# Query features interleaved over the partitions and moved in three wide transfers, row maxima turned by one transpose

## The reference

```python
# layer 0: differential attention, 32 half-heads of 8, softmax over 77 keys
q = layernorm(x) @ Wq.T; k = ctx @ Wk.T; v = ctx @ Wv.T
att = softmax(einsum('bhtd,bhnd->bhtn', q, k) * 8 ** -0.5)      # 32 half-heads
att = att[:, :, 0] - lam * att[:, :, 1]                          # 16 heads
x = x + tanh(g) * einsum('bhtn,bhnd->bhtd', att, v)
x = x + tanh(g) * (mixture of top 3 of 8 experts, gelu)(layernorm(x))
# layer 1: 16 heads of 16, the same Wq (with its bias) for q, k and v
att = softmax(einsum('bhqd,bhkd->bhqk', q, k) / 4)
x = x + tanh(g) * ((att @ v) @ Wo + bo)
x = x + tanh(g) * (silu(h @ Wg) * (h @ Wu)) @ Wd                 # h = layernorm(x)
```

## Time and profile before

| | |
|---|---|
| median of 3 runs | 671.64 us (671.02 to 672.87) |
| the profiled execution's own time | 671.35 us |
| its span in the trace | 669.6 us |
| TensorE (PE) busy | 608.3 us, 91% |
| VectorE (DVE) busy | 384.5 us, 57% |
| ScalarE (ACT) busy | 361.6 us, 54% |
| GpSimd (POOL) busy | 148.2 us, 22% |
| mean granted TensorE clock | 0.985 |

### The profile page before, as it was taken

How to read it: one execution, slowest core, us unless ns; L and a number is a source line. 1 busy time by engine, 2 the same in 40 slices (tenths; PEclk the granted TensorE clock), 3 DMA queues, 4 the chain that set the end, 5 groups by cost and what they waited for, 6 DMA issues and landing times.

```text
span 669.6 us, 11648 instructions
## 1 busy us (share of the span) xinstructions
PE 608.3 (91%) x4364; PEld 503.0 (75%) x4364; DVE 384.5 (57%) x813; ACT 361.6 (54%) x615; POOL 148.2 (22%) x218
## 2 busy tenths in 40 slices
PE   2688888898899999999999999999778998999998
PEld 2565555554599899999999888899656776878887
DVE  6668676887753524434555434534486663656654
ACT  4345757686765746546557435535675433443421
POOL 9716265354630000000000000000564210210000
PEclk9789999999999999999999999999999998999999
DMA  7302120222030030300312340020132100000000
GB/s 226 107 12 88 35 62 8 49 51 97 32 126 1 10 117 1 118 9 1 126 25 72 80 142 2 2 95 2 44 99 65 35 1 0 34 1 22 12 33 31
DMA packets 22551, 34.76 MB, mean 52 GB/s; under 512 B 4704, under 2 KB 13280, under 8 KB 22496
## 3 DMA queue, kind: packets, MB, share of 16 engines
q1 hardware_dynamic: 20224, 30.51, 14.7%
q0 software_dynamic: 1984, 3.44, 2.2%
q10 hardware_dynamic: 288, 0.07, 0.0%
HBM read 18.93 MB, written 2.10 MB: 31 GB/s over the span
## 4 chain that ended last, share of the span: by engine, by line
PE 73%; DVE 10%; ACT 5%; issue 4%; POOL 3%; DMA 1%; ACTq 0%; DVEq 0%; POOLq 0%
PE PV L1259 21%; PE SC L1287 21%; PE SC L1259 9%; PE PV L1278 4%; PE AUX L1259 4%; DVE NM L1134 3%; PE SC L1406 3%; PE AUX L1368 3%; PE PV L1287 2%; PE AUX L1287 2%; DVE O L1142 2%; ACT PB L906 2%; ACT XN L851 1%; PE AUX L1326 1%; POOL RSTD L716 1%
## 5 line engine op out<-in xcount | busy, mean ns | idle before, releaser
L992 DVE TENSOR_TENSOR HL<-HF,HH 128x512 fp32r<-128x512 f32 x96 | 67.2, 700 | 154.6 <-ACT HH L948 154.4
L906 ACT ACTIVATE PB<-SC 77x1024 f32<-77x1024 f32 x96 | 95.2, 1014 | 50.1 <-PE SC L1406 49.8
L1287 PE MATMUL SC<-WBH,HL 128*128 128x256 f32 x384 | 108.7, 283 | 0.0
L1287 PE MATMUL SC<-WBL,HH 128*128 128x256 f32 x384 | 108.6, 283 | 0.0
L1287 PE MATMUL SC<-WBH,HH 128*128 128x256 f32 x384 | 108.6, 283 | 0.0
L948 ACT ACTIVATE HH<-PV 128x512 fp32r<-128x512 f32 x96 | 57.3, 596 | 72.1 <-PE SC L1287 72.1
L943 ACT ACTIVATE HF<-PV 128x512 f32<-128x512 f32 x96 | 57.3, 597 | 54.7 <-PE PV L1259 52.7
L716 POOL TENSOR_TENSOR RSTD<-RSTD,NHALF 128x4 f32<-128x4 f32 x16 | 17.8, 1115 | 291.5 <-DVE RSTD L1066 291.4
L1259 PE MATMUL PV<-XH,WAH 128*128 128x512 f32 x192 | 77.6, 404 | 1.0 <-DVE O L1142 1.0
L1287 PEld LDWEIGHTS SC<-WBL,HH 128*128 128x128 f32 x384 | 72.7, 189 | 3.9
L1287 PEld LDWEIGHTS SC<-WBH,HH 128*128 128x128 f32 x384 | 72.5, 189 | 4.0 <-DVE HL L992 0.3
(11 more groups left out here) (254 smaller groups left out, 1228.7 us busy)
## 6 DMA issues: line engine op xcount, KB each, us to landing
QG<-QH SPq DMA_DIRECT2D x96, 64.0 KB, 2.0
WSA<-in_wa SPq DMA_DIRECT2D x6, 1024.0 KB, 4.8
WSB<-in_wb SPq DMA_DIRECT2D x12, 512.0 KB, 6.4
QG<-QL SPq DMA_DIRECT2D x48, 64.0 KB, 2.0
X<-in_x SPq DMA_DIRECT2D x4, 512.0 KB, 6.0
QG<-QH POOLq DMA_DIRECT2D x32, 64.0 KB, 2.3
out_x<-X SPq DMA_DIRECT2D x8, 256.0 KB, 2.1
QG<-QL POOLq DMA_DIRECT2D x16, 64.0 KB, 2.3
```

The source lines that it names most:

```text
L906: act.activation(probs(n)[0:S, :, :], scores(n)[0:S, :, :], ACT.Exp, scale=SCALE[a]).then_inc(exp_done, 1)
L992: return dve.tensor_tensor(dst, raw, hi.bitcast(F32), ALU.subtract)
L1287: ins = pe.matmul(ps[:, D * (t % 2):D * (t % 2 + 1)], lhs[:, block], rhs, start=first and t == 2 * i and n == 0, stop=last and t == 2 * i ...
```

## The change

1. The columns of both `Wq` (and the bias per feature) are put in another order on the host: feature `4r + g` of a half is row `r` of group `g`. So the four groups of a half lie interleaved over the 128 partitions, and one DMA of 128 rows x 512 fills 32 rows of all four groups. A half takes 3 DMAs in place of 12. In the pairs of `BOTH` the third is issued by GpSimd's queue, which waits for `QH` alone.
2. `NM` has the heads outside and the blocks inside, `NM[:, n % 2, h, t]`, so that one transpose turns heads x blocks (64, 32 or, in attention 1, 32 columns) at once. ScalarE copies a bank of up to 64 rows x 128, and the DMA to `QG` reads 16 (or 8) rows of 128 for each group.
3. `WDH` and `WDL` for layer 1 must have the groups in the old order: the copies and subtractions read `WQ1R` with a step of four elements, four instructions each in place of one on ScalarE and two on GpSimd. The products of `keys(1, 3)` and `keys(1, 4)` read `WQ1H` and `WQ1L` with a step of four elements as moving operand.

```diff
         SG = [at(f"SG{i}", [P, NT], F32, wq_at + 4096 + 2048 * i) for i in range(2)]
-        NM = place("NM", [P, 2, TT, HEADS[0]], F32)
-        NMT = place("NMT", [P, NT], F32R)
+        NM = place("NM", [P, 2, HEADS[0], TT], F32)
+        NMT = place("NMT", [P, P], F32R)
         ident = place("ident", [P, P], F32)
...
         def query_moved(eng, n, c):
-            eng.wait_ge(q_moved[n % 2][c], 16 * sum(6 if m in BOTH else 12 for m in range(n % 2, n + 1, 2)))
+            eng.wait_ge(q_moved[n % 2][c], 16 * sum(2 if m in BOTH else 3 for m in range(n % 2, n + 1, 2)))
             if n in BOTH:
-                eng.wait_ge(pool_moved[n][c], 16 * 6)
+                eng.wait_ge(pool_moved[n][c], 16)
+
+        def by_group(raw, c, h):
+
+            return (raw[:, c, P * h:P * (h + 1)].rearrange("p (r g) -> p g r", g=G // KC)
+                    .unsqueeze(2).to_broadcast([P, G // KC, 3, 32]))
         def ffn_half(i, h):
...
                 return ap.rearrange("(c p) n -> p c n", p=P)
+
+            def move_maxima(queries, a, g, at_g):
+
+                return sp.dma_start(queries[ROWS:ROWS + NS[a], g, :].bitcast(F32),
+                                    NMT[at_g:at_g + NS[a] * TT, :].bitcast(F32))
             sp.dma_start(X[:, 0:TT, :], x[0]).then_inc(x_in[0], 16)
...
                     used(sp, ("query", a, j, c))
-                    for r in range(2 if n in BOTH else 4):
-                        for q, src in enumerate((QH, QL, QH)):
-                            sp.dma_start(QG[n % 2][32 * q:32 * q + 32, 4 * c + r, :].bitcast(F32),
-                                         src[32 * r:32 * r + 32, c, :].bitcast(F32)).then_inc(q_moved[n % 2][c], 16)
+                    for q, src in enumerate((QH, QL) if n in BOTH else (QH, QL, QH)):
+                        sp.dma_start(QG[n % 2][32 * q:32 * q + 32, G // KC * c:G // KC * (c + 1), :].bitcast(F32),
+                                     src[:, c, :].bitcast(F32)).then_inc(q_moved[n % 2][c], 16)
                 elif kind == "negmax":
...
                     for g in range(G // KC):
-                        at_g = 32 * c + NS[a] * g
-                        sp.dma_start(QG[n % 2][ROWS:ROWS + NS[a], G // KC * c + g, :].bitcast(F32),
-                                     NMT[at_g:at_g + NS[a], :].bitcast(F32)).then_inc(m_moved[n % 2][G // KC * c + g], 16)
+                        move_maxima(QG[n % 2], a, G // KC * c + g,
+                                    64 * c + NS[a] * TT * g).then_inc(m_moved[n % 2][G // KC * c + g], 16)
                 elif kind == "negpart":
...
                     for g in (2 * p, 2 * p + 1):
-                        at_g = 64 * p + NS[0] * (g % 2)
-                        sp.dma_start(QG[0][ROWS:ROWS + NS[0], g, :].bitcast(F32),
-                                     NMT[at_g:at_g + NS[0], :].bitcast(F32)).then_inc(m_moved[0][g], 16)
+                        move_maxima(QG[0], 0, g, 64 * p + NS[0] * TT * (g % 2)).then_inc(m_moved[0][g], 16)
                 elif kind == "zone_load":
...
                         pool.wait_ge(sc_ready, unit((n - 2) // J, (n - 2) % J, 0) + units[(n - 2) // J] * (c + 1) // KC)
-                    used(pool, ("query", a, j, c))
-                    for r in range(2, 4):
-                        for q, src in enumerate((QH, QL, QH)):
-                            pool.dma_start(QG[n % 2][32 * q:32 * q + 32, 4 * c + r, :].bitcast(F32),
-                                           src[32 * r:32 * r + 32, c, :].bitcast(F32)).then_inc(pool_moved[n][c], 16)
+                    filled(pool, ("query", a, j, c))
+                    pool.wait_ge(qh_ready, order["query", a, j, c] + 1)
+                    pool.dma_start(QG[n % 2][2 * 32:3 * 32, G // KC * c:G // KC * (c + 1), :].bitcast(F32),
+                                   QH[:, c, :].bitcast(F32)).then_inc(pool_moved[n][c], 16)
                 elif kind == "weights_split" and step[1] == 2:
...
                     lo_part(WQ1L[:, :, :], WQ1R[:, :, :], WQ1H[:, :, :]).then_inc(split1_done, 1)
-                    pool.wait_ge(split_hi, 6)
+                    pool.wait_ge(split_hi, 9)
                     for c in range(KC):
-                        lo_part(WDL[:, c, :, :, :],
-                                WQ1R[:, c, :].rearrange("p (g r) -> p g r", r=32).unsqueeze(2).to_broadcast([P, G, 3, 32]),
-                                WDH[:, c, :, :, :]).then_inc(split1_done, 1)
+                        for h in range(KC):
+                            gs = slice(G // KC * h, G // KC * (h + 1))
+                            lo_part(WDL[:, c, gs, :, :], by_group(WQ1R, c, h), WDH[:, c, gs, :, :]).then_inc(split1_done, 1)
                 elif kind == "weights_split" and step[1] == 0:
...
                     filled(act, ("keys", 0, 4, 0))
-                    dup_hi(WQ1R)
+                    for c in range(KC):
+                        for h in range(KC):
+                            act.activation(WDH[:, c, G // KC * h:G // KC * (h + 1), :, :], by_group(WQ1R, c, h),
+                                           copy).then_inc(split_hi, 1)
                 elif kind == "weights_split":
...
                             act.wait_ge(m_moved[(n - 1) % 2][g], 16 * ((n - 1) // 2 + 1))
-                    n_heads = HEADS[a] // KC
-                    act.activation(NMT[32 * c:32 * c + n_heads, :], bank(step + (0,))[0:n_heads, :], copy).then_inc(frees(step + (0,)), 1)
+                    rows = HEADS[a] // KC * TT
+                    act.activation(NMT[64 * c:64 * c + rows, :], bank(step + (0,))[0:rows, 0:P], copy).then_inc(frees(step + (0,)), 1)
                 elif kind == "negpart":
...
                     filled(act, key)
-                    act.activation(NMT[at_p:at_p + 8, :], bank(key)[0:8, :], copy).then_inc(frees(key), 1)
+                    act.activation(NMT[at_p:at_p + 32, :], bank(key)[0:32, 0:P], copy).then_inc(frees(key), 1)
                 elif kind == "attend":
...
                     filled(dve, key)
-                    dve.tensor_reduce(NM[:, n % 2, t, h:h + k], bank(key)[:, 0:k * S].rearrange("p (h n) -> p h n", h=k),
+                    dve.tensor_reduce(NM[:, n % 2, h:h + k, t], bank(key)[:, 0:k * S].rearrange("p (h n) -> p h n", h=k),
                                       AX_X, ALU.max, negate=True).then_inc(frees(key), 1)
...
                 return ins
+            def turn_maxima(ps, maxima):
+
+                rows = maxima.shape[1] * TT
+                return pe.transpose(ps[0:rows, 0:P], maxima.rearrange("p h t -> p (h t)"), ident[:, :])
+
             def attend_values(a, j, k):
...
                         else:
-                            pe.wait_ge(split1_done, 3)
+                            pe.wait_ge(split1_done, 5)
                     ps = fill(step + (0,))
...
                         cols = slice((i - 3) * S, (i - 2) * S)
-                        ins = product(ps[0:S, 0:D], [(CH[:, c, cols], CL[:, c, cols], vh[:, c, :], vl[:, c, :])
-                                                     for c in range(KC)])
+                        if a == 0:
+                            vh, vl = (tuple(w[:, c, :] for c in range(KC)) for w in (vh, vl))
+                        else:
+                            vh, vl = (tuple(w[:, c, :].rearrange("p (k r g) -> p k g r", k=KC, g=G // KC)
+                                            for c in range(KC)) for w in (vh, vl))
+                        ins = product(ps[0:S, 0:D], [(CH[:, c, cols], CL[:, c, cols], vh[c], vl[c]) for c in range(KC)])
                     ins.then_inc(aux_ready, 1)
...
                     ps = fill(step + (0,))
-                    for t in range(TT):
-                        ins = pe.transpose(ps[0:8, P * t:P * (t + 1)], NM[:, 0, t, 8 * p:8 * p + 8], ident[:, :])
-                    ins.then_inc(aux_ready, 1)
+                    turn_maxima(ps, NM[:, 0, 8 * p:8 * p + 8, :]).then_inc(aux_ready, 1)
                 elif kind == "negmax":
...
                     ps = fill(step + (0,))
-                    for t in range(TT):
-                        ins = pe.transpose(ps[0:n_heads, P * t:P * (t + 1)],
-                                           NM[:, (J * a + j) % 2, t, n_heads * c:n_heads * (c + 1)], ident[:, :])
-                    ins.then_inc(aux_ready, 1)
+                    turn_maxima(ps, NM[:, (J * a + j) % 2, n_heads * c:n_heads * (c + 1), :]).then_inc(aux_ready, 1)
                 elif kind == "attend":
...
     bq = np.asarray(inputs["L1_xattn_bq"])
+
+    def by_row(w):
+        return w.reshape(-1, KC, G // KC, 32).transpose(0, 1, 3, 2).reshape(w.shape)
+
     arrays = {
...
         "g_x": inputs["g_xattn"], "g_f": inputs["g_ffn"],
-        "wq0": np.asarray(inputs["L0_xattn_Wq"]).T, "wk0": np.asarray(inputs["L0_xattn_Wk"]).T,
+        "wq0": by_row(np.asarray(inputs["L0_xattn_Wq"]).T), "wk0": np.asarray(inputs["L0_xattn_Wk"]).T,
         "wv0": np.asarray(inputs["L0_xattn_Wv"]).T,
...
         "wa": inputs["L0_ffn_Wa"], "wb": inputs["L0_ffn_Wb"],
```

(8 more changed lines are left out.)

## The result

The changed kernel takes 680.83 us (median of 6 runs) beside 671.46 us for the kernel before (6 runs). One of the six took 1704.97 us, a slow execution; without it the median is 679.94 us, and the ratio, which leaves it out too, is 1.0121, interval 1.0102 to 1.0141: slower by 1.2%, where I had forecast 667.4 us and given slower 0.10. The profiled execution took 681.76 us, its span is 680.0 us, 10.4 us above that of before.

A forecast was written before the change was run, and what follows sets the result against it. It took TensorE to bound the expert stage and a chain changing hands the attentions. Savings of 5.2 us, less 0.55 for the split and 0.5 for strided reads, gave -4.2: 671.64 to 667.4 us, range 664.0 to 671.0.

The forecast's parts named there:

- The query transfers: Query halves moved to QG: each there 1 to 5 us earlier, but hidden; value 0, bounds -0.2 and 0.
- Nothing queued behind the issues on SyncE is late: SyncE's queue: the maxima's transfer starts when its copy ends, so query issues do not delay it; no cost.
- The transfer of the maxima: Maxima's DMA, 1.86 us twice on the chain: 512 B pieces cost between 0 and +0.2 each; taken as 0.
- The transposes and the copies: Maxima on TensorE and ScalarE: fewer transposes save 1.18 and 2.05 us, shorter copies 2.3; 5.2 after taking off 0.3.
- rival 2: Attentions: the next wait takes the savings, only start and expert stage keep theirs; -2.0 us, 669.6 to 670.6; chance 0.19.
- The dearer split: GpSimd's WDL for layer 1: four pieces of 1.04 us, 4.15 against 3.60, +0.55 us straight on the chain.
- Reads with a step of four: The 12 matmuls of keys(1, 3) and keys(1, 4): a doubling, +1.4 us, of which +0.5 on the chain.
- rival 3: Split and layer-1 value products: step-of-four reads are dear, +8.8 against -5.2, 675.2 us, slower; chance 0.10.
- rival 4: TensorE from 42 to 48 us: full clock comes later, up to 5.4 us more, +1.2 net, 672.8 us; chance 0.03.

The follow-up runs named there:

- e8: The changed kernel with its three merged query transfers a half written to every third row of QG, not 32 neighbouring rows; output not the reference's; 669.66 us, ratio 0.9960.
- e3: The changed kernel with each half's queries moved in 12 transfers of 64 KB that read every fourth row; 670.81 us, ratio 0.9978 to the kernel before.
- e1: The kernel before with the turned maxima only (one transpose, copies of 128 columns, maxima's transfers in 512 B rows); 669.71 us, ratio 0.9959.
- e6: e1 with its one transpose done four times over into the same place; ratio 0.9973 to the kernel before.
- e2: The changed kernel without the turned maxima (four transposes and the old copies again); 685.15 us, ratio 1.018 to the kernel before.
- e9: e1 with 16 matmuls of 512 columns, whose result nobody reads, ahead of the first maximum; ratio 0.9964 to the kernel before.
- e10: The kernel before with 16 matmuls of 512 columns, whose result nobody reads, ahead of the first maximum; ratio 1.0007.
- m1: Separate kernel without computation, timing transfers between SBUF rows form by form and in bursts; 256 KB from 128 rows into 32 neighbouring rows took 3.97 us.
- m2: Second transfer-only kernel, with further 256 KB forms differing in rows and piece size; 128 rows into 32 rows that lie four apart took 2.38 us.

## Why the prediction was wrong, step by step

- **The query transfers: this step failed.** "A half is there 1 to 5 us earlier" was wrong in sign for the first half, and with it the value 0. I took the landing of one transfer (3 to 4.5 us; 3.97 measured for one alone) as its whole cost, and forgot that they share the engines: the six of pair 0, both halves, are issued within 3 us, what counts at the start is when the last one of the first half lands, and it took 9.34 us. With the same six in well-spread rows (e8) it took 5.28. My own row gave the warning: the wait of 4.5 us had two causes within 0.15 us of each other, so any growth of the transfer came out one for one. I priced a gain there and no loss. The bounds -0.2 and 0 had no row behind the upper one, since no transfer of this form was in the trace.
- **"Nothing queued behind the issues on SyncE is late".** I looked at when the maxima's transfer is issued, not at what it shares. It landed after 5.28 in place of 1.86 us, +3.4 on the chain. **The transfer of the maxima** by itself was right: 1.96 in e3, +0.1.
- **The transposes and the copies**: the pieces are as forecast (17 in place of 68; 0.27 us; copies 0.26 us against 0.30). Their worth was not: 2.8 us by e1 in place of 5.2. The expert stage gave 1.2 us, what follows 0.6, together the 1.8 by which the span shrank (669.6 to 667.8). In the expert stage I had counted three copies, 0.9 us; e6 shows them at nothing. Attention 0 gave nothing back, the first expert matmul is at 178.9 us in e1 as before, but the savings of its start did appear: at the first key product of layer 1, e1 is 2.03 us ahead (87.93 against 89.96), 0.54 of it by an earlier first maximum. They went again where TensorE ran at the lower clock, as the item on the clock shows. So the sum is near that of rival 2 (-3.0 for transposes and copies), and by luck: rival 2 kept the start's savings and named a second path, not the clock, for the rest.
- **The dearer split**: the term was mis-sized. GpSimd's pieces take 1.18 us and not 1.04, 4.61 against 3.60 us: +1.0 in place of +0.55. The pieces are 14% above my estimate, which took the step of four at nothing; no run has them without the step, so whether the step or the estimate is to blame is not shown.
- **Reads with a step of four** by TensorE: near the doubling that I took. Three of these matmuls in the kernel after start 0.23 us apart, where it was 0.12:

```profile
118.77 0.41 PE L1267 MATMUL PV<-WQ1H,CH 128*77 128x256 f32 x1
119.00 0.41 PE L1267 MATMUL PV<-WQ1L,CH 128*77 128x256 f32 x1
119.23 0.41 PE L1267 MATMUL PV<-WQ1H,CL 128*77 128x256 f32 x1
```

  12 x 0.11 = 1.3 us against my 1.4; the granted clock is 1.00 over these matmuls in both kernels. The rule of the Trainium skill ("Advanced Engine Details and Errata", "Memory Cachelines") that I had weighed is right in sign, and not dear enough for rival 3. Both terms together, +1.05 forecast, are 1.3 us by e3 less e1. The reductions that write `NM` with that step are unchanged (475 and 480 ns in e1, 473 and 479 before).
- **The clock** (rival 4, chance 0.03): it came true in part, beside the main cause. Its sign was a clock below 0.64 behind 27 us. It is 0.50 from 27.6 to 39.5 us in the kernel after, and as low in e1, e3 and e8, which have the turned maxima but no late first maximum, while e6, with four transposes again, has 0.64. (e2, with four transposes and the late first maximum, has 0.50 too, so in the kernel after both may lower it.) The first key product of layer 1 took 1.77 us before, 2.56 in e1 and 3.17 in e3, against 3.16 in the kernel after (from the chains of before, e1 and e3, in this order):

```profile
89.96 1.77 PE AUX L1259 x18
...
87.93 2.56 PE AUX L1259 x18
...
89.86 3.17 PE AUX L1269 x18
```

  e3 has no wide transfer, so these 1.4 us are no part of the 9.6. In e1 the product costs 0.8 us of the 2.03 by which e1 was ahead. The rest goes between 132.64 and 136.73 us, at a granted clock of 0.55 (to 136.16 us) where before has 1.00; the largest piece, from the chain of e1, took 1.04 us before:

```profile
134.29 1.87 PE PV L1283 x16
```

  At 136.73 us e1 and before stand level. So the clock took attention 0's savings in e1's trace: 0.8 and 1.5 us, together 2.3, near the 2.2 that rival 4 named. I had given that rival 0.03, and e9 and e10 do not rule it out. Each of these is one traced execution, and why the clock fell at those places is not shown.

The differences in a row are -2.8 (turned maxima, e1), +1.3 (split and strided reads, e3 less e1) and +9.6 (form of the transfers, the kernel after less e3). They add up to the +8.1 us measured (1.0121 x 671.46 - 671.46) because each run starts where the last one ends; the sum proves nothing by itself. Without the wide form, the forecast by the same terms would have been right in sign and 2 to 3 us too good.

Of the versions that compute the reference, e1 is the fastest: 669.71 us, 0.9959. A wide form with the keys in interleaved rows as well, e8 made whole, wasn't built.

## What to carry to other kernels

Before you merge DMAs, look at which rows of SBUF the merged one writes and reads, not only at the issues it saves: 12 transfers of 64 KB were cheaper here than three of 256 KB of the same bytes, where 128 source rows went into 32 neighbouring ones; the same three into rows spread over the partitions cost nothing (e8). In the windows, read the DMA share together with the GB/s; a full share at half of the rate is a transfer that is badly placed. And where one wait has two causes within a few tenths, price both as if each stood on the path.

## What the runs showed of the hardware

- 256 KB between rows of SBUF: 2.3 to 2.4 us where the rows lie over all 128, 3.0 to 3.3 from rows 0 to 31 into the same rows, 3.6 from 32 into 128, 3.9 to 4.0 from 128 into rows 0 to 31 or 0 to 63 (m1, m2).
- A transfer of 8 KB behind three such wide ones in the same queue: 6.14 us; issued from another engine's queue together with the first of them: 4.51; behind twelve narrow ones: 1.96 (m1, m2).
- TensorE with a moving operand of fp32 in steps of four: 0.23 us for 256 columns against 0.12. GpSimd's subtraction with one such operand: 1.18 us for 384 elements, against 1.04 estimated from the earlier trace rows without the step. VectorE writing four to six values in such steps: no change.
